# A fourth piece buffer in the table stage, and node records gathered behind a tile's second piece

## The reference, cut to what matters

```
k, q, v = typed_linear(x, ntype, Wk / Wq / Wv)         # a weight per node type
kT = einsum('nhd,htdo->nhto', k, Watt)                 # all 32 edge types for every node
vT = einsum('nhd,htdo->nhto', v, Wmsg)
kw, m = kT[src, :, etype], vT[src, :, etype]           # per edge
a = sum(kw * q[dst]) * pri / 4;  att = edge_softmax(a, dst)
hag = segment_sum(m * att, dst);  h = silu(typed_linear(hag, ntype, Wa)) ... skip, norm
```

## Time and profile before

| | |
|---|---|
| runs, us | 5927.63, 5916.28, 5936.7 (median 5927.63) |
| span of the profiled execution | 5930.1 us; the page has no other time for it |
| table stage of layer 0 | 142.5 (first copy) to 757.7 us (last landing) |
| table stage of layer 1 | 2942.0 to 3545.8 us |
| busy over the span | PE 66%, POOL 66%, DVE 60%, ACT 28% |
| busy share of the 16 DMA engines | 9 tenths in the slices of the table stages, 6 in those of the edge stages |

### The profile page before, as it was taken

One profiled execution on the slowest core, in us unless ns is written; L12 is line 12 of the kernel. 1 busy time (PEld: TensorE's weight loads), 2 busy tenths in 40 slices (PEclk: granted clock), 3 DMA queues, 4 the chain that ended last, 5 costly groups with the idle time before them and its releaser, 6 DMA issues. The chain is left out here.

```text
span 5930.1 us, 75994 instructions
## 1 busy us (share of the span) xinstructions
PE 3888.4 (66%) x19279; PEld 2908.1 (49%) x19280; DVE 3581.7 (60%) x6760; ACT 1663.9 (28%) x4125; POOL 3928.0 (66%) x3959
## 2 busy tenths in 40 slices
PE   2888856666666666665388876666666666666524
PEld 1322346665655655555233335555555555556414
DVE  3554556666666666665666656666666666666657
ACT  0444511111111111111366651222222222222226
POOL 4556467777777777776133337777777777777565
PEclk8888866667666676667688986667766776666656
DMA  7999866666666666666388976666667666666511
GB/s 127 385 355 369 361 197 190 186 183 188 188 187 184 185 184 189 185 183 170 101 360 357 378 294 175 185 186 189 187 185 187 185 191 186 185 185 188 153 40 34
DMA packets 413476, 1234.48 MB, mean 208 GB/s; under 512 B 169651, under 2 KB 222903, under 8 KB 362130
## 3 DMA queue, kind: packets, MB, share of 16 engines
q0 software_dynamic: 202768, 852.28, 44.2%
q1 hardware_dynamic: 121302, 144.14, 12.4%
q10 hardware_dynamic: 89044, 234.66, 10.6%
HBM read 576.49 MB, written 726.60 MB: 220 GB/s over the span
## 5 line engine op out<-in xcount | busy, mean ns | idle before, releaser
L1150 POOL DMA_INDIRECT kv_e_<-table_d,row_s_ x1568 | 1541.1, 983 | 485.1 <-issue 480.3
L1150 POOL DMA_INDIRECT kv_e<-table_d,row_s x1568 | 1536.7, 980 | 491.8 <-issue 486.0
L1331 PE MATMUL sum_ps<-pv,to_rank 128*128 128x136 f32 x3136 | 622.8, 384 | 149.7 <-DVE pv L1244 149.7
L1331 PE MATMUL sum_ps_<-pv_,to_rank_ 128*128 128x136 f32 x3136 | 614.7, 381 | 149.5 <-DVE pv_ L1244 149.5
L1331 PEld LDWEIGHTS sum_ps<-pv,to_rank 128*128 128x128 f32 x3136 | 603.6, 288 | 178.0 <-issue 178.0
L1331 PEld LDWEIGHTS sum_ps_<-pv_,to_rank_ 128*128 128x128 f32 x3136 | 595.5, 285 | 177.8 <-issue 177.8
L1297 PE MATMUL qe_ps<-q_w,of_rank 128*128 (+1 forms) x3168 | 536.6, 327 | 155.9 <-DVE kq L1223 122.7
L1297 PE MATMUL qe_ps_<-q_w_,of_rank_ 128*128 (+1 forms) x3168 | 530.6, 326 | 126.0 <-DVE kq_ L1223 100.4
L1223 DVE TENSOR_TENSOR kq<-kv_e,qe_ps 128x512 f32<-128x512 f32 x392 | 267.6, 683 | 523.0 <-DMA kv_e<-table_d,row_s 522.9
L1223 DVE TENSOR_TENSOR kq_<-kv_e_,qe_ps_ 128x512 f32<-128x512 f32 x392 | 267.8, 683 | 521.1 <-DMA kv_e_<-table_d,row_s_ 521.0
L1297 PEld LDWEIGHTS qe_ps<-q_w,of_rank 128*128 128x128 f32 x3168 | 469.9, 230 | 211.0 <-issue 180.2
(11 more groups left out here) (402 smaller groups left out, 6488.5 us busy)
## 6 DMA issues: line engine op xcount, KB each, us to landing
part_d<-sums ACTq DMA_DIRECT2D x105, 1088.0 KB, 4.8
part_d<-sums_ ACTq DMA_DIRECT2D x98, 1088.0 KB, 4.8
local_b<-local_d SPq DMA_DIRECT2D x100, 512.0 KB, 6.2
local_b_<-local_d SPq DMA_DIRECT2D x100, 512.0 KB, 5.6
kv_e<-table_d,row_s POOLq DMA_INDIRECT x1568, 2.8
kv_e_<-table_d,row_s_ POOLq DMA_INDIRECT x1568, 2.8
q_w<-q_d SPq DMA_DIRECT2D x100, 64.0 KB
q_w_<-q_d SPq DMA_DIRECT2D x100, 64.0 KB
```

The costliest lines, as they stand in the source:

```text
L1150: pool.indirect_dma_start(out=kv_e[:, b, t, :], out_offset=None, in_=table_d, in_offset=bass.IndirectOffsetOnAxis(ap=row_s[:, b, t:t + 1], ...
L1331: last = pe.matmul(sum_ps[:, n % 3, (t - t0) * REC:(t - t0 + 1) * REC], to_rank[:, b, t, :], pv[:, b, t, :], start=True, stop=True)
```

## The change

`RING` goes from 3 to 4, in both layers: the copies of a piece wait for the piece four before. `landed`, the count from which the semaphores of the ring start in layer 1, becomes a list, since 114 pieces don't divide by four. In layer 0 `beside` is called behind both pieces of a tile: of a tile's three edge gathers, the first and third are issued behind piece 0 and the second behind piece 1; a group's node records are gathered behind piece 1 of tile `ROWS_AT[g] - 1`, not behind its piece 0; q is scattered behind piece 0 as before. No instruction of PE, DVE or ACT changes its place or its work.

```
-RING = 3
+RING = 4
...
-            landed = l * 16 * (NPC * NS // RING)
+            landed = [l * 16 * len(range(r, NPC * NS, RING)) for r in range(RING)]
...
-                def beside(n):
-
-                    for k in range(EDGES_AT[n], EDGES_AT[n + 1]):
+                def beside(n, c):
+
+                    edge_tiles = range(EDGES_AT[n], EDGES_AT[n + 1])
+                    for k in edge_tiles[c::NPC]:
                         gather_edges(k)
                     for g in range(NGP):
-                        if n == ROWS_AT[g] - 1:
+                        if c == 1 and n == ROWS_AT[g] - 1:
                             gather_nodes(g)
-                        if n == ROWS_AT[g]:
+                        if c == 0 and n == ROWS_AT[g]:
                             scatter_kept_q(g)
...
-                        if c == 0 and not l:
-                            beside(n)
+                        if not l:
+                            beside(n, c)
...
-                if i % (UNITS // NPC) == 0 and landed + 16 * (m // RING):
-                    eng.wait_ge(s_piece[m % RING], landed + 16 * (m // RING))
+                if i % (UNITS // NPC) == 0 and landed[m % RING] + 16 * (m // RING):
+                    eng.wait_ge(s_piece[m % RING], landed[m % RING] + 16 * (m // RING))
```

More of the change, by code:

```diff
@@ L855, in _ @@
                 for r in range(RING):
-                    pool.wait_ge(s_piece[r], landed + 16 * (NPC * NS // RING))
+                    pool.wait_ge(s_piece[r], landed[r] + 16 * len(range(r, NPC * NS, RING)))
                 for r in range(3):
```

## The result

| | before | changed |
|---|---|---|
| median of 12 runs, us | 5932.44 | 5949.48 |
| lowest to highest | 5916.28 to 5939.66 | 5934.72 to 5964.15 |
| ratio, 95% interval | | 1.0031 (1.0020 to 1.0042) |
| span of the profiled execution | 5930.1 | 5954.5 |
| table stage of layer 0, first copy to last landing | 615.2 | 659.3 |

A forecast was written before the change was run, and what follows sets the result against it. Transfers on the fullest DMA engine bound the table stages, with room only at late pieces. Layer 0 +21.5 us and layer 1 -12 us gave +9.5 us on 5927.6, so 5937 us, range 5913 to 5960.

The forecast's parts named there:

- the first rival: Whole kernel: run-ahead of the engines hides the moved node gathers; -25 us, 5902 us; chance 0.12.
- Bound by the slowest DMA engine, with room only at late pieces: Table stages: fullest engine idles only at late pieces, 8.3 us together in layer 0, 10.7 us in layer 1.
- Layer 1, -12 us: Layer 1's table stage: fourth buffer removes two thirds of late time, -7 us, and shortens the end, -5 us.
- Tiles 0 to 22, 0 us: Layer 0, tiles 0 to 22: no piece late, so the fourth buffer gives nothing and moved edge gathers cost nothing.
- A group's chain: Layer 0 groups, T the landing of (n-1, 1): bytes at T+7.5, cover to T+5.8; pairs +8 us, singles +5 us.
- The piece (n+1, 1): Layer 0 pairs: 0.4 us lost behind the second group's scatters; groups standing alone had no such loss.
- The end, +8.5 us: End of layer 0's stage: copies of (53, 1) start 4.9 us later, and tile 56 adds 3.6 us.
- No gain in layer 1: Layer 1: late pieces are the engines' own pace or the transfer rate's limit; only layer 0's +21.5 stands, 5949; chance 0.12.
- buffer unused: Both layers: fourth buffer is never reached, the move costs only its tail; 0 to +5 us, 5930; chance 0.05.
- Run-ahead hides the move: Layer 0: records land soon enough for (n, 1), gaining 8.3 us and 5 at the end; total -25 us; chance 0.12.
- The stall costs more than the cover shows: Layer 0's 19 groups: DVE's stall slows PE and following copies, 14 us more; total +23, 5951; chance 0.16.
- The signs named beforehand: Trace signs: longer cast waits and three-tile times in layer 0; landing median near 15 us, four or five late in layer 1.

The follow-up runs named there:

- e1: Changed kernel with all gathers back behind piece 0, so four buffers alone: 5908.04 us, ratio 0.9947 to the kernel before.
- e2: Changed kernel with RING = 3, so gathers spread with three buffers: 5975.11 us, ratio 1.0062 to the kernel before.
- e4: Changed kernel with node gathers two pieces earlier (first group as before the change): 5886.76 us, ratio 0.9917 to the kernel before.
- e3: Changed kernel with node gathers back where they stood before, four buffers and edge gathers spread: 5917.22 us, ratio 0.9967 to the kernel before.
- e5: Changed kernel with node gathers one piece later, behind the first piece of the group's own tile: 6042.18 us, ratio 1.0175 to the kernel before.

## Why the prediction came out, point by point

- **The whole.** Forecast was +9.5 us, slightly slower; measured +17, within the range. The mechanism, its places and both signs were right. Both layers' sums were about half of the measured ones, and the errors went against each other, so that the total came this near is in part luck. (Half of the first rival would also have put the lower edge of the range at 5915, not 5913.)
- **Bound by the slowest DMA engine, with room only at late pieces.** Right as a picture, too narrow as a count. I counted pieces that landed about 7.1 us behind their issue. The count gave 10.7 us for layer 1; the fourth buffer took 12.5 us there up to (52, 1) (mean of the six kernels with four buffers, 562.2, against the three with three, 574.7). A landing time of 7.1 us marks only a piece that finds an empty queue. A piece issued less than 2.1 us ahead of the landing before it comes late too.
- **Layer 1, -12 us.** Mis-sized: -18.7 us as a mean of those kernels (580.8 against 599.5), -24.3 between the two traces; the trace of before has the longest stage of the three with three buffers. Two thirds of the late time was too careful, and the end gave 6.4 us (18.5 against 24.3 to 25.9), where I took 5.
- **Tiles 0 to 22, 0 us.** Wrong by 7 us. The waits for edges came (10.6 us) and cost little, but the fourth buffer gave 3 to 7 us where no piece had been counted as late. In what way it saves them no run isolates.
- **A group's chain.** Its times were right: with T at 470.6, the issue of (n, 1) at T+5.4 (476.01) and that of (n+1, 0) at T+12.0 (482.57). The cover was mis-sized. I had credited the six small transfers with 0.8 us behind (n, 0), but it landed at T+5.1, not T+5.8. So (n, 1) loses 2.6 us as a mean of the seven pairs where I had 1.65, and (n+1, 0) 1.3 where I had 1.1. The sum for the pairs had a slip too. It took off 2.0 us in each of seven pairs, 14 us, for what was lost at (n, 1) before, while my own count had 8.3 us there; the seven landings give 10.9. With 8.3 the forecast for the pairs would have been +14 and the total +15. Cover and slip are 8 of the 18 us by which the pairs were forecast too low, and the cover 3 of the 8 us at the single groups.
- **The piece (n+1, 1).** It was put at 0.4 us in a pair and at nothing behind a single group. In the changed kernel it lands 7.9 us behind (n+1, 0), 6.6 before, as means of the seven pairs: +9.0 us in the pairs, where 2.8 were forecast, and +4.7 at the three single groups. Tile 30 shows two parts. (30, 1) is issued at 488.67, only 0.95 us ahead of the landing of (30, 0), so with 2.1 us to its first bytes 1.15 us are lost. And one DMA engine falls behind: of the 16 increments of the piece's semaphore, one from each engine, seven come at 495.7 to 495.8 and the last at 497.8. In the kernel before they come at 493.0 to 493.2 and 494.9, the same lag without the late issue. The two parts, 1.15 and 2.0 us, are what (30, 1) takes over 5.0. The lag is also what I had read as small transfers. I left 1.9 us per three tiles for 15 of them; between the landings of (29, 1) and (32, 1) it lies in (30, 1) alone, 7.2 us where 5.0 is usual, and the four pieces around it take 4.9 to 5.0 each.
- **The rest.** 3 us in the pairs, mostly at (25, 1) and (28, 1), and 1 us at the single groups aren't attributed.
- **The end, +8.5 us.** Nearly right: +12.1. The two waits were where they were predicted. The copies behind a stall came slower: the fourth copy of (53, 1) waited 0.97 us for PE, and the next piece 1.79.
- **No gain in layer 1, or buffer unused** are refuted by e1 and by 8.8 us of waits for buffers where there were 51.1. **Run-ahead hides the move** is refuted by layer 0's stage, 44.1 us longer, and by e2, where the loss is the same without the fourth buffer. **The stall costs more than the cover shows** was the nearest rival: its 23 us in total wasn't reached by the medians, but layer 0 alone passed its +36.
- **The signs named beforehand.** Three tiles took 37.2 us (35 forecast), the last issue came 36.0 us behind the landing of (52, 1) (34). The casts waited 5.8 us each and at most 9.2 (8 to 13). In layer 1 the median from issue to landing up to (52, 1) is 10.6 us, 9.3 before over the same pieces, and not near 15, so the queue seldom held as many pieces as four buffers allow. Two or three pieces are late there, not four or five.

That records land with the piece ahead of them is what four kernels vary. With four buffers and spread edges, the node gathers stand one piece later each time in e4, e3, the changed kernel and e5, and the stage takes 589.9, 613.3, 659.3 and 752.7 us. The last step takes away the last piece of cover and is 4.9 us per group, one piece's transfer. The steps before are 1.2 and 2.4 us per group, since part of the chain was still covered. The Trainium skill, "DMA: Bandwidth & Descriptors", section "Queues, rings and completion order", says in its paragraph on the queues of SyncE and ScalarE that each DMA engine takes descriptors in ring order. The transfers here are GpSimd's, and the trace agrees for them: node gathers took 9.2 to 10.5 us behind a piece, and 2.1 us at the least (the shortest of the 57 in layer 0).

## What to carry to other kernels

A buffer more raises how far the engines run ahead, but a small load on the same queue limits it too: what counts is the number of transfers queued behind the load when it lands, against everything that the issuing engine has to do from then to the next large transfer. Write down that chain in full, other small issues included, before moving a load. Look also for what the loads wait for themselves (in e1 a write of the records, 7.4 us). Here, with four buffers and spread edges, the same node gathers cost 46 us in layer 0 one piece later and gave 23 us one piece earlier; the version with four buffers and early gathers (e4) is 0.8% faster than the kernel before.

## What was not expected of the hardware

Small transfers issued between pieces don't fill the gap that a late piece leaves: behind three scatters the gap was 2.5 us, where their own time had been put at 0.4.

And one of the 16 DMA engines falls behind the others by 1 to 2.2 us in one piece and stays behind. In the kernel before it is so at (13, 1) (seven increments at 305.7 to 305.8, the last at 307.2) and at (30, 1) (493.0 to 493.2, and 494.9, though the piece wasn't late). Behind (30, 1) the lag stays for the next pieces at 1.5 to 1.7 us, until all 16 engines end (32, 1), a late piece, within 0.2 us of one another. So a piece that lands late seems to cost twice, its own gap and the lag that comes anew in a piece behind it; in e4, where no piece is late, (n+1, 1) takes 5.7 us in the pairs and 4.9 at the single groups. That is a reading of the traces, not tested by a run. In layer 1, (13, 1) took 5.0 us because the lag of 1.8 us was already there at (13, 0). No run tells why one engine falls behind.
